# Recurrence: the scaling of v by beta as eight ScalarE activations in place of one VectorE multiplication

## The reference

```python
v = hidden_states @ Wv
beta = jax.nn.sigmoid(hidden_states @ Wb + bb)
q = silu(causal_dwconv(q, qconv_w, qconv_b))     # k likewise, then a layer norm of both
def step(S, inp):
    q_t, k_t, v_t, b_t = inp
    b = b_t[..., None, None]
    S = (1.0 - b) * S + b * (v_t[..., :, None] * k_t[..., None, :])
    o_t = jnp.einsum('bhvk,bhk->bhv', S, q_t)
    return (S, o_t)
```

## Time and profile before

| what | value |
|---|---|
| median of three runs | 2673.86 us |
| the profiled execution's own time | 2663.39 us |
| its span in the profile | 2661.6 us |
| TensorE busy | 2517.4 us, 95% of the span |
| VectorE busy | 1813.9 us, 68% |
| ScalarE busy | 1082.2 us, 41% |
| GpSimd busy | 847.6 us, 32% |
| mean granted TensorE clock | 0.978 |

### The profile page before, as it was taken

One profiled execution on the slowest core, in us unless ns is written; L12 is line 12 of the kernel. 1 busy time (PEld: TensorE's weight loads), 2 busy tenths in 40 slices (PEclk: granted clock), 3 DMA queues, 4 the chain that ended last, 5 costly groups with the idle time before them and its releaser, 6 DMA issues. The chain is left out here.

```text
span 2661.6 us, 43731 instructions
## 1 busy us (share of the span) xinstructions
PE 2517.4 (95%) x15296; PEld 2224.4 (84%) x15296; DVE 1813.9 (68%) x3332; ACT 1082.2 (41%) x1513; POOL 847.6 (32%) x442
## 2 busy tenths in 40 slices
PE   4899899999999999999999999997899999999997
PEld 4688788889988988889898898997788887888886
DVE  5679899988888988889888898888431212433232
ACT  5444454444434444444444444444432322422221
POOL 2145445434433434334343434344100000121220
PEclk8899999999999999999999999999999999999999
DMA  7555555654445464444456444453471101441320
GB/s 279 175 171 176 167 191 168 221 190 151 162 142 167 158 222 158 143 153 156 152 192 202 151 155 146 158 183 121 153 237 48 58 37 43 136 154 48 110 83 27
DMA packets 232189, 395.55 MB, mean 149 GB/s; under 512 B 58358, under 2 KB 159990, under 8 KB 219130
## 3 DMA queue, kind: packets, MB, share of 16 engines
q1 hardware_dynamic: 125946, 192.21, 22.0%
q10 hardware_dynamic: 97408, 176.71, 19.7%
q0 software_dynamic: 8704, 25.19, 3.1%
HBM read 304.88 MB, written 97.55 MB: 151 GB/s over the span
## 5 line engine op out<-in xcount | busy, mean ns | idle before, releaser
L1008 DVE SCALAR_TENSOR_TENSOR xn_rows<-ps_proj,conv,xn_rows 128x1021 f32<-128x1021 f32 x381 | 486.9, 1278 | 11.6 <-ACT xn_rows L895 2.5
L1185 PE MATMUL ps_proj<-xt_hi,w_hi 128*128 128x512 f32 x1008 | 418.9, 416 | 38.4 <-DVE rc_v_beta L1061 27.4
L1187 PE MATMUL ps_proj<-xt_hi,w_lo 128*128 128x512 f32 x1008 | 403.0, 400 | 0.0
L1186 PE MATMUL ps_proj<-xt_lo,w_hi 128*128 128x512 f32 x1008 | 402.0, 399 | 0.0
L786 POOL TENSOR_TENSOR rc_k_state<-rc_tok_k,k_norm_rows 128x1024 f32<-128x1024 f32 x64 | 153.5, 2399 | 638.5 <-DVE rc_q_silu L1052 554.7
L1207 PE MATMUL ps_proj<-wv_hi,xt_hi 128*128 128x256 f32 x1024 | 295.3, 288 | 0.6 <-PEq L75 0.6
L1208 PE MATMUL ps_proj<-wv_lo,xt_hi 128*128 128x256 f32 x1024 | 289.8, 283 | 0.0
L1209 PE MATMUL ps_proj<-wv_hi,xt_lo 128*128 128x256 f32 x1024 | 289.6, 283 | 0.0
L1185 PEld LDWEIGHTS ps_proj<-xt_hi,w_hi 128*128 128x128 f32 x1008 | 194.2, 193 | 80.4 <-DVE rc_v_beta L1061 29.8
L1187 PEld LDWEIGHTS ps_proj<-xt_hi,w_lo 128*128 128x128 f32 x1008 | 193.5, 192 | 43.9
L1186 PEld LDWEIGHTS ps_proj<-xt_lo,w_hi 128*128 128x128 f32 x1008 | 194.3, 193 | 36.6
(11 more groups left out here) (181 smaller groups left out, 5762.8 us busy)
## 6 DMA issues: line engine op xcount, KB each, us to landing
rc_q_rows<-scratch_q_rows ACTq DMA_DIRECT2D x64, 1024.0 KB
rc_decay_all<-scratch_decay ACTq DMA_DIRECT2D x64, 512.0 KB, 3.7
rc_cum_all<-scratch_cum ACTq DMA_DIRECT2D x64, 512.0 KB, 4.1
scratch_o<-rc_o_sb ACTq DMA_DIRECT2D x64, 512.0 KB, 4.9
w_hi<-scratch_w_split SPq DMA_DIRECT2D x48, 512.0 KB, 4.0
w_lo<-scratch_w_split SPq DMA_DIRECT2D x48, 512.0 KB, 5.2
wv_hi<-scratch_wv_split SPq DMA_DIRECT2D x24, 512.0 KB, 3.9
wv_lo<-scratch_wv_split SPq DMA_DIRECT2D x24, 512.0 KB, 5.0
```

The costliest lines, as they stand in the source:

```text
L1008: nc.vector.scalar_tensor_tensor(out=act_cm[j][:, back:], in0=projected[:, 0:L - back], scalar=conv[par][:, j, t:t + 1], in1=act_cm[j][:, ...
L1185: nc.tensor.matmul(out, hi, xt_hi[:, k, cols], start=k == 0, stop=False)
L1186: nc.tensor.matmul(out, hi, xt_lo[:, k, cols], start=False, stop=False)
L1187: last = nc.tensor.matmul(out, lo, xt_hi[:, k, cols], start=False, stop=k == KC - 1)
```

## The change

The multiplication leaves VectorE's list. In its place ScalarE does eight activations of 128x128, one for each of the four chunks and two heads, between its silu of q and its silu of k. Each reads 128 columns of `ps_proj` and multiplies by a scale that is one number per partition, taken from `beta_steps`. The two waits of the multiplication (v projected; the outputs that last read this half of the buffer) go with it, and an instruction that only carries a wait (`stand`, L46) is added before the eight, since the address of the scale is computed in registers in the loops. The eighth activation counts up `v_beta_done`. The products are the same.

```diff
@@ ScalarE, step
+                def gate_values():
+
+                    after_step(act, "v_projected", B_.i)
+                    after_step(act, "outputs_mm", 2 * B_.pair - 3)
+                    stand(act, keep["carrier_sp"])
+                    first = B_.par * VC
+                    for c in range(VC):
+                        for h in range(2):
+                            columns = slice((2 * c + h) * P, (2 * c + h + 1) * P)
+                            last = nc.scalar.activation(
+                                v_beta[B_.pair_par][:, first + c, h], ps_proj[:, B_.par, columns], ACT.Identity,
+                                scale=keep["beta_steps"][:, first + c, bass.ds(B_.pair * 2 + h, 1)])
+                    last.then_inc(S["v_beta_done"], 1)
+
                 if B_.live:
                     silu(0)
+                    gate_values()
                     silu(1)
@@ VectorE, step
-                def gate_values():
-
-                    after_step(dve, "v_projected", B_.i)
-                    after_step(dve, "outputs_mm", 2 * B_.pair - 3)
-                    first = B_.par * VC
-                    gate = keep["beta_steps"][:, first:first + VC, bass.ds(B_.pair * 2, 2)].unsqueeze(3)
-                    nc.vector.tensor_tensor(v_beta[B_.pair_par][:, first:first + VC],
-                                            ps_proj[:, B_.par].rearrange("p (c h t) -> p c h t", h=2, t=P),
-                                            gate.to_broadcast([P, VC, 2, P]), ALU.mult
-                                            ).then_inc(S["v_beta_done"], 1)
-
-                if B_.live:
-                    gate_values()
```

## The result

The changed kernel takes **2626.77 us** (median of 4 runs, 2624.82 to 2633.23), beside 2672.62 us (2669.6 to 2676.84, 4 runs) for the kernel before on the same chip. The ratio is 0.9832, with a 95% interval of 0.981 to 0.9854: 46 us less. The forecast was 2638 us, in a range of 2624 to 2680. The profiled execution of the changed kernel took 2626.93 us, its span 2625.1.

The account below looks back on a forecast made before the run. TensorE bounds the kernel, losing 41 us around waits for the scaled v at trip starts. Removing these (-41), late activations (+10) and first-sequence relief (-5) give -36 from 2673.9: 2638 us, range 2624 to 2680.

Parts of the forecast that it names:

- What bounded the kernel: TensorE sets the end; its 10 waits for the scaled v, behind VectorE's 6.3 us branch gap, cost 41 us.
- The eight: ScalarE's eight activations a step take 2.21 us; v comes late in two of four steps, costing some 10 us.
- slow clock: TensorE's granted clock at 0.50 instead of 1.00 behind 8 of 10 waits; none charged behind the new short waits.
- the 63 us lost: By the skill's rule of multiplications on VectorE alone, 64 x 0.99 us would make the kernel 63 us slower.
- The gap goes: VectorE's 6.28 us gap at its loop branch ends, as its trip gets shorter: 31 us saved before relief; chance 0.46.
- Gap stays: Rival: VectorE's branch gap remains, now before the scan; 26 us saved with relief, 2648 us; chance 0.22.
- ScalarE gets the gap: Rival: ScalarE's longer trip pays VectorE's gap at its branch, v comes later; 26 us lost, 2700 us; chance 0.15.
- The eight as long as L965's: Rival: the eight activations last 3.19 us; 2675 us, no change; chance 0.12 together with other losses that cancel the gain.
- Relief in the first sequence: TensorE waits less for VectorE's shift and convolution there: 5 us taken, between bounds of 0 and 15 us.
- The sum: Whole kernel: -41 + 10 - 5 = -36 us, from the median of 2673.9 to 2638 us.
- the low end of the range: The eight take 1.47 us and are never late (-41), with some 9 us of relief: about -50, 2624 us.

Follow-up runs that it names:

- run 1: The kernel before, multiplication still on VectorE, with 60 small instructions that only count up an unused semaphore ahead of VectorE's steps: 2630.86 us, ratio 0.9855.
- run 8: The changed kernel with 24 small instructions that do nothing ahead of VectorE's steps: 2661.36 us, ratio 0.9973.
- Run 7: The changed kernel with the eight activations only in the first sequence's 16 steps and VectorE's multiplication in all later steps: 2621.6 us, ratio 0.9819.
- run 2: The changed kernel with 40 small instructions that do nothing ahead of VectorE's steps: 2645.57 us, ratio 0.9908.
- run 4: The changed kernel with small instructions that do nothing on ScalarE, 57 ahead of its steps and 8 in each step: 2697.74 us, ratio 1.0109.
- run 3: The changed kernel with the eight activations behind ScalarE's silu of k instead of between the two silus: 2657.18 us, ratio 0.9956.
- 9: The changed kernel with 32 small instructions that do nothing ahead of VectorE's steps: 2644.29 us, ratio 0.991.

## Why the prediction was right, and where it was off

*What bounded the kernel.* Right. The 41 us at the trip starts, charged to VectorE's gap, are what run 1 gets back without moving anything (40 us by the medians; 38.8 in the profiled recurrence, 1726.2 against 1687.4).

*The eight.* Right: 2.15 us measured, 2.21 forecast; each of them takes 0.343 to 0.415 us in the trace, 0.359 forecast. Late at the trip start by 0.56 us (k's projection comes 6.94 us into the step, 1168.91 - 1161.97, and 6.38 where nothing is late), 0.64 forecast; in the third step by 0.04 to 0.18, 0.26 forecast. The forecast charged 10 us for this. The trace shows 5.1 us of waits, and with them away steps 16 to 64 were 8.3 us shorter in one profile of each kernel. No slow clock stands behind waits this short, as forecast (1.00 in the window above). The Trainium skill (ScalarE: Activation LUTs, Rules for kernel authors) gives multiplications to VectorE. Per step the trace agrees (1.14 us against 2.15). Once the gap is out of the way, the two engines are worth the same here as far as is shown (2630.9 and 2626.8 us, some 5 us of the first being run 1's small instructions): neither the 63 us lost that were worked out for that rule, nor a gain.

*The gap goes.* Right, and this choice carried the forecast. Its reason was half right, and the rest was luck. The few instructions by which the trip ran over did decide, but that the trip became 14 places shorter would not have been enough: 291 instructions from place 92 would end at 382, and run 8, which ends at 381, has the gap. What helped was that the code ahead of the loop became 25 places shorter as well; the prediction named that only in passing. Run 7 shows that these 25 suffice: its trip has all 305 instructions, begins at 67 like that of the changed kernel, and has no gap. The Trainium skill (Runtime: NRT & Kernel Launch, Instruction fetch mechanics) speaks of a window of two blocks of 256 instructions. The trace agrees that a branch out of what is held has to fetch, but a trip of 291 is free or costs 6 to 7.5 us according to its place alone, in packets of 128.

*Gap stays* (2648 us, 26 saved): run 2 made this case, with 25 saved, 2645.6.

*ScalarE gets the gap* (2700 us, 26 lost): run 4 made it, with 27 lost, 2697.7. The price was nearly right (some 5 of the 27 us are the small instructions ahead), the way to it only in part: the prediction let v be late, but TensorE needs the silu of q for the turn before it needs v, and most of the wait (37.8 us) stands there.

*The eight as long as L965's* (2675 us, 37 over the forecast): run 3 brings v some 4.1 us after the silu's start (one silu more, then 2.15 us), nearly as this rival had it (4.20), and the price of a trip was right (4.0 us). The 7 us charged to the first sequence weren't lost there, and the kernel came out 30 us over the changed one.

*Relief in the first sequence.* 5 us forecast. The steps of the first sequence were shorter with the work moved by 6 to 12 us where the gap stands (426.7 before; 420.3, 418.8 and 414.7 in runs 2, 8 and 9) and by 3 to 6 where it doesn't (418.6 in run 1; 415.7 and 412.8 in two profiles of the changed kernel). With one profile of each kernel that keeps the multiplication, the size stays open.

*The sum.* -36 forecast, -46 by the medians, -41 in the profiled recurrence. The step that was mis-sized is the charge of 10 us for the eight being late, nearer 5 to 8; with it the first sequence gave 11 us where relief and its share of trip starts were forecast at some 8. What remains is of the size of the scatter: in the six profiles without small instructions ahead the recurrence's first turn of q comes anywhere from 110.6 to 115.7 us, and the profiled execution of the kernel before lies 9 us below its median. All the same the forecast level of 2638 lay 11 us too high, and the measured time 2.8 us above the low end of the range.

## What to carry to other kernels

An "issue" gap of some microseconds at the head of a loop's trip, with an instruction packet in it, was here a matter of where the trip lies in the engine's stream: before moving work for its sake, shift the stream by a few dozen instructions that do nothing, and see what is left to gain. Any edit that adds or removes instructions on an engine with a loop can make or break such a gap (VectorE's in run 1, ScalarE's in run 4), so a change is judged fairly only by the two kernels without it (here 4 us by the medians, not shown apart from none, and not 46). The small instructions of such a test have a price of their own, to be read from the trace (some 5 us for 60 of them in run 1). And a consumer that overwrites a buffer in halves can wait for half of the work that reads it: the waits went, though a gain of the whole kernel isn't shown.

## What the runs showed of the hardware

The price of the gap was known from the earlier trace rows, its rule was not. With the gap, 86 to 90 packets of instructions are read in a run by this queue; without, 31 to 33, and in the changed kernel none at all in two whole trips (1058 to 1270 us), against 10 in two trips of the kernel before (1074.5 to 1293). In the trace's records of the kernel before, the packet of the branch's target begins to arrive 4.3 us after the branch (1183.75 to 1188.03 us), and the first instruction runs 1.8 us after that. I had not expected the gap to come while the branch still stands some places ahead of the border, nor that this is the worst of the places tried: 2661 us with 24 more instructions, 2644 with 32, 2645.6 with 40.
